# A two-layer hybrid network on one core: the loops of all stages written out, and the normalisation of the MoE route stages moved from VectorE to ScalarE

## The reference

```python
x = x + rwkv(layernorm(x))            # L0_attn_a: token shift, low-rank mixes, recurrence over time
x = x + moe(layernorm(x))             # L0_ffn: 8 experts, each takes its top 65 tokens of a sequence
x = x + retention(layernorm(x))       # L0_attn_b: 16 heads, decay, gated
x = x + moe(layernorm(x))
x = x + rnn(layernorm(x))             # L1_attn_a: h = tanh(h @ A.T + bx_t), 256 steps
x = x + ffn(layernorm(x))             # L1_ffn: 128 -> 512 -> 128, gelu
x = x + wkv(layernorm(x))             # L1_attn_b: 1024 channels, cumulative sums
x = x + ffn(layernorm(x))

def _layernorm(x, axis=-1, eps=1e-05):
    m = jnp.mean(x, axis=axis, keepdims=True)
    v = jnp.var(x, axis=axis, keepdims=True)
    return (x - m) / jnp.sqrt(v + eps)

scores = softmax(einsum('bsd,ed->bse', x, router_w))      # of the MoE block
gate_vals, sel_idx = top_k(swapaxes(scores, 1, 2), 65)
```

## Time and profile before

| | us |
|---|---|
| median of 3 runs | 3743.26 (3743.24 to 3748.52) |
| the profiled execution, own time | 3741.77 |
| its span, first to last instruction | 3740.0 |
| mean granted TensorE clock | 0.879 |

### The profile page before, as it was taken

How to read it: one execution, slowest core, us unless ns; L and a number is a source line. 1 busy time by engine, 2 the same in 40 slices (tenths; PEclk the granted TensorE clock), 3 DMA queues, 4 the chain that set the end, 5 groups by cost and what they waited for, 6 DMA issues and landing times. The chain is left out here.

```text
span 3740.0 us, 56099 instructions
## 1 busy us (share of the span) xinstructions
PE 3132.0 (84%) x16680; PEld 2027.5 (54%) x16680; DVE 2491.7 (67%) x5841; ACT 1666.5 (45%) x3563; POOL 1202.9 (32%) x1203
## 2 busy tenths in 40 slices
PE   4777776599987399999649996887979999999989
PEld 2333334488853144444548885676745555555557
DVE  5888777544469677777564444201569999999975
ACT  1222221233333299999413332221436666666644
POOL 2333332000013277777310000100224444444432
PEclk9878876699988599999769998555989999999999
DMA  3000001111013200000220000000000000000001
GB/s 106 1 0 0 0 0 52 63 44 43 0 40 110 65 28 27 27 27 19 69 76 35 35 17 1 1 0 25 0 1 1 1 0 0 0 0 0 0 1 45
DMA packets 106211, 89.75 MB, mean 24 GB/s; under 512 B 15789, under 2 KB 95923, under 8 KB 103776
## 3 DMA queue, kind: packets, MB, share of 16 engines
q1 hardware_dynamic: 104784, 87.13, 7.2%
q10 hardware_dynamic: 1296, 1.02, 0.1%
HBM read 57.68 MB, written 30.15 MB: 23 GB/s over the span
## 5 line engine op out<-in xcount | busy, mean ns | idle before, releaser
L2228 ACT ACTIVATE m_x_hT<-m_x_hid,wm_b 128x260 f32<-128x260 f32 x512 | 242.3, 478 | 435.3 <-PE m_x_hid L2150 435.3
L1112 DVE TENSOR_REDUCE c_tM<-c_tpa 128x2 f32<-128x512 f32 x512 | 331.8, 681 | 129.7 <-PE c_tpa L1014 128.7
L1229 POOL TENSOR_TENSOR c_tE<-c_tE,c_tDm 128x256 f32<-128x256 f32 x512 | 372.6, 728 | 139.6 <-ACT c_tE L1189 124.9
L1189 ACT ACTIVATE c_tE<-c_tpb 128x512 f32<-128x512 f32 x512 | 310.1, 607 | 43.2 <-PE c_tpb L1031 43.2
L2150 PE MATMUL m_x_hid<-m_x_xg,wm_w 128*128 128x260 f32 x1024 | 306.6, 387 | 8.4 <-ACT m_x_hT L2228 6.1
L2158 PE MATMUL m_x_yp<-m_x_hT,wm_w 128*128 128x260 f32 x1024 | 299.9, 382 | 0.0
L79 POOL TENSOR_TENSOR rstd<-vareps,neg_half 128x4 f32<-128x4 f32 x105 | 112.7, 1073 | 550.7 <-DVE vareps L68 550.7
L1565 POOL TENSOR_TENSOR b_wkv<-b_at,b_rec 128x512 f32<-128x512 f32 x128 | 163.0, 1274 | 314.1 <-DVE b_rec L1501 314.1
L1014 PE MATMUL c_tpa<-c_tK,c_Qm 96*128 96x256 f16 x1024 | 205.2, 283 | 48.8 <-DMA c_Qm<-aug_d 34.2
L72 DVE TENSOR_SCALAR xn<-X,mean,rstd 128x128 f32 (+1 forms) x420 | 162.9, 449 | 108.2 <-POOL rstd L79 108.2
L2075 DVE TENSOR_SCALAR m_x_yT<-m_x_yp,wm_b 128x260 f32<-128x260 f32 x128 | 62.5, 489 | 251.3 <-PE m_x_yp L2158 251.3
(11 more groups left out here) (296 smaller groups left out, 7371.1 us busy)
## 6 DMA issues: line engine op xcount, KB each, us to landing
m_x_ir<-idx_d SPq DMA_DIRECT2D x16, 1040.0 KB, 6.7
xn_d<-xn SPq DMA_DIRECT2D x32, 256.0 KB, 2.3
m_x_xs<-xn_d SPq DMA_DIRECT2D x16, 512.0 KB, 4.1
c_tK<-k_d SPq DMA_DIRECT2D x32, 192.0 KB
c_Qm<-q_d SPq DMA_DIRECT2D x128, 48.0 KB
wm_w<-in_m_w SPq DMA_DIRECT2D x2, 2048.0 KB, 10.2
gate_d<-c_pgate SPq DMA_DIRECT2D x16, 256.0 KB
q_d<-c_phi SPq DMA_DIRECT2D x32, 128.0 KB
```

The source lines that it names most:

```text
L1112: nc.vector.tensor_reduce(out=M[:, u % 2, 2 * h:2 * h + 2], in_=pa[:, h % 2], axis=AX.X, op=ALU.max).then_inc(s["max_done"], 1)
L1189: nc.scalar.activation(E[:, h % 8].rearrange("p a q -> p (a q)"), pb[:, h % 2, :], ACT.Exp).then_inc(s["exp_done"], 1)
L1229: nc.gpsimd.tensor_tensor(diag, diag, Dm[:, u % 2, h:h + 1, :].to_broadcast([P, 2, P]), ALU.mult).then_inc(s["dmul_done"], 1)
L2228: nc.scalar.activation(hT[:, e % 2, j, :], hid[:, c % 2, 0:QW], ACT.Gelu, bias=w["m_b1"][:, c:c + 1]).then_inc(s["gelu_done"], 1)
```

## The change

All 29 `Fori` loops become Python loops, so every engine's code is written out. And in the route stage, besides:

- ScalarE normalises: `activation(Identity, scale=rstd, bias=shift)` with shift = -mean * rstd, four to a group, in the order evac(g), normalise(g + 2);
- VectorE only does `moments`, for all 16 groups one after another; the mean comes out negated;
- GpSimd works out shift behind the power, and now waits before the power until ScalarE has normalised group g - 2, whose slot it overwrites;
- moments(g) waits for `shift_done` of group g - 2 in place of `xn_done`; ScalarE's normalise(g) waits for shift(g), for the turn of group g - 2 and for the store of group g - 2.

```diff
-            with dve.Fori(1, NG // 2) as i:
+            for i in range(1, NG // 2):
...
@@ stage_route @@
+        shift = sb("shift", [P, 2, GT])
...
             def moments(g, u):
 
                 at_least(dve, s["ln_tick"], g * MOMENTS)
-                at_least(dve, s["xn_done"], (g - 1) * GT)
+                at_least(dve, s["shift_done"], g - 1)
...
-                nc.vector.tensor_scalar(mean[:, u, :], mean[:, u, :], 0.5, None, ALU.mult).then_inc(s["ln_tick"], 1)
+                nc.vector.tensor_scalar(mean[:, u, :], mean[:, u, :], -0.5, None, ALU.mult).then_inc(s["ln_tick"], 1)
...
-            def normalise(g, u, wait):
-                if wait:
-                    dve.wait_ge(s["turned"], g - 1)
-                    dve.wait_ge(stored[u], (g - u) * 8)
-                dve.wait_ge(s["ln_rstd"], g + 1)
-                for i in range(GT):
-                    nc.vector.tensor_scalar(k.xn[:, u, i, :], k.X[:, g * GT + i, :], mean[:, u, i:i + 1], rstd[:, u, i:i + 1],
-                                            ALU.subtract, ALU.mult).then_inc(s["xn_done"], 1)
-
-            moments(0, 0)
-            for u in range(2):
-                moments(u + 1, 1 - u)
-                normalise(u, u, False)
-            with dve.Fori(1, NG // 2) as i:
-                for u in range(2):
-                    g = i * 2 + u
-                    moments(g + 1, 1 - u)
-                    normalise(g, u, True)
+            for g in range(NG):
+                moments(g, g % 2)
...
                     pool.wait_ge(s["ln_tick"], (g + 1) * MOMENTS)
+                    at_least(pool, s["xn_done"], (g - 1) * GT)
                     nc.gpsimd.tensor_tensor(rstd[:, u, :], vareps[:, u, :], k.neg_half[:], ALU.pow).then_inc(s["ln_rstd"], 1)
+                    pool.wait_ge(s["ln_rstd"], g + 1)
+                    nc.gpsimd.tensor_tensor(shift[:, u, :], mean[:, u, :], rstd[:, u, :], ALU.mult).then_inc(s["shift_done"], 1)
...
-            evac(0, 0, False)
-            evac(1, 1, False)
-            with act.Fori(1, NG // 2) as i:
-                for u in range(2):
-                    evac(i * 2 + u, u, True)
+
+            def normalise(g, u):
+                act.wait_ge(s["shift_done"], g + 1)
+                at_least(act, s["turned"], g - 1)
+                at_least(act, stored[u], (g - u) * 8)
+                for i in range(GT):
+                    nc.scalar.activation(k.xn[:, u, i, :], k.X[:, g * GT + i, :], ACT.Identity, scale=rstd[:, u, i:i + 1],
+                                         bias=shift[:, u, i:i + 1]).then_inc(s["xn_done"], 1)
+
+            normalise(0, 0)
+            normalise(1, 1)
+            for g in range(NG):
+                evac(g, g % 2, g > 1)
+                if g + 2 < NG:
+                    normalise(g + 2, g % 2)
```

More of the change, by code:

```diff
@@ L243, in _ @@
             down(1, 1, False)
-            with pe.Fori(1, NG // 2) as i:
+            for i in range(1, NG // 2):
                 for u in range(2):
@@ L488, in _ @@
             iteration(1, 1, False)
-            with pool.Fori(1, NG // 2) as i:
+            for i in range(1, NG // 2):
                 for u in range(2):
@@ L782, in _ @@
             one(0)
-            with pool.Fori(1, NG) as g:
+            for g in range(1, NG):
                 one(g)
@@ L1091, in _ @@
                 iteration(0, u, first=(u == 0), second=(u == 1))
-            with pe.Fori(1, NI - 1) as i:
+            for i in range(1, NI - 1):
                 for u in range(NB):
@@ L1233, in _ @@
                 iteration(0, u)
-            with pool.Fori(1, NI - 1) as i:
+            for i in range(1, NI - 1):
                 for u in range(NB):
@@ L1806, in stage_route @@
     with ExitStack() as ctx:
-        s = sems(nc, ctx, tag, "ln_tick ln_rstd xn_done turned xT_ready logits stored0 stored1 soft exp_done rows work top0 top1 out")
+        s = sems(nc, ctx, tag, "ln_tick shift_done ln_rstd xn_done turned xT_ready logits stored0 stored1 soft exp_done rows work top0 top1 out")
         ps = lambda name, shape: ctx.enter_context(nc.psum_tensor(tag + name, shape, F32))
@@ L1832, in _ @@
         def _(sp):
-            with sp.Fori(0, NG // 2) as i:
+            for i in range(0, NG // 2):
                 for u in range(2):
@@ L1923, in _ @@
         def _(pool):
-            with pool.Fori(0, NG // 2) as i:
+            for i in range(0, NG // 2):
                 for u in range(2):
@@ L1947, in _ @@
             turn_in(1, 1, False)
-            with pe.Fori(0, NG // 2 - 1) as i:
+            for i in range(0, NG // 2 - 1):
                 for u in range(2):
@@ L2047, in _ @@
             low_part(1, 1)
-            with pool.Fori(1, NQ // 2) as i:
+            for i in range(1, NQ // 2):
                 for u in range(2):
@@ L2119, in _ @@
             quad(1, 1, False, False)
-            with dve.Fori(1, NQ // 2 - 1) as i:
+            for i in range(1, NQ // 2 - 1):
                 for u in range(2):
@@ L2205, in _ @@
             quad(1, 1, False, False)
-            with pe.Fori(1, NQ // 2 - 1) as i:
+            for i in range(1, NQ // 2 - 1):
                 for u in range(2):
@@ L2233, in _ @@
             quad(1, 1, False, False)
-            with act.Fori(1, NQ // 2 - 1) as i:
+            for i in range(1, NQ // 2 - 1):
                 for u in range(2):
```

9 lines of the change are left out of this document (4 added, 5 removed).

## The result

The changed kernel takes **3714.3 us** (median of 4 runs, 3713.1 to 3716.3) against 3745.7 for the kernel before (3743.2 to 3748.5, 4 runs): ratio 0.9916, 95% interval 0.9901 to 0.9932. Predicted were 3722 us (3704 to 3735) and faster with a chance of 0.86. The sign and the range held; the gain between the medians is 31 us where 20 were forecast.

A forecast was written before the change was run, and what follows sets the result against it. VectorE was taken to pace the route stage at 3.07 us a group, TensorE to bound wkv and FFN. Route 14, project 2.9, experts 1.3 and rwkv 2 sum to 20 us off 3741.8: 3722 us, range 3704 to 3735.

The forecast's parts named there:

- Route: Both route stages: pace falls from VectorE's 3.07 us a group to TensorE's 2.62; 7 us a stage, 14 us.
- TensorE's pitch: Route stage: turns 0.91 plus logits 1.71 make 2.62 us a group, the true pitch some 0.05 less.
- Project: Retention project: written out 9.33 us a group against 9.54 looped; 2.9 us gained.
- Experts: Both experts stages: written out 44.46 us a quad against 44.61 looped; 1.3 us gained.
- Attend and FFN: Retention attend, 15.68 us looped and written out, and both FFN stages, bound by TensorE: 0 gained.
- wkv: wkv stage: TensorE is busy 97% and its queue hides the loop arithmetic; 0 gained.
- rwkv: rwkv stage, bound by a chain through four engines at 34.13 us an iteration: 2 us gained from written-out loops.
- A: Route stages: TensorE's clock rises, ScalarE's 2.2 us sets the pace, 13 us more, 3709 us; chance 8%.
- B: rwkv stage: leaves its 34.13 us period for a mean near 33.3, 11 us more, 3711 us; chance 15%.
- C: Route: ScalarE or GpSimd binds at 2.9 us a group, 3730 us (8%); if rwkv also loses, 3737 (7%).
- E: Loops: removing registers shows only in peeled prologues and rwkv gives nothing, 3729 us; within the forecast's range, no separate chance.
- D: Written-out code: 76 new instruction fetches stall TensorE, 71 us more, 3793 us; with every second one 3757; chance 5%.

The follow-up runs named there:

- before + 64: The kernel before with 64 one-column memsets added in VectorE's idle time in the recurrence stage: 3782.6 us (2 runs).

## Why the prediction was right, and where it was off

**Route, 7 us a stage: right mechanism, mis-sized, 9.4 and 9.1.** VectorE set the pace before and TensorE does now, at a clock of 0.50. The term that was off most is TensorE's pitch: "2.62", with 0.05 taken off for the modelled end of the last matmul. It measured 2.45, 0.17 less. From start to start, a turn is 0.89 us and the logits 1.56, where the forecast had 0.91 and, to a modelled end, 1.71. The 0.12 a group that were missed are 1.8 us a stage; another 0.5 is the lead to the first turn, which grew by 0.35 us and not by 0.9 (4.49 before, 4.84 now). Together they are the 2.4 by which 9.4 exceeds 7. The idle time told it as well: 8.0 us of waits over 16 groups are 0.5 a group, 3.07 - 0.5 = 2.57, and there too the ends are modelled. Of the parts, ScalarE's normalisation was 0.40 an operation and measured 0.484; two overlap by a little, so a group is 1.65 us as forecast (1.6). GpSimd's multiply was 0.4 and measured 0.21, inside its bounds. The new waits cost 0.6 us of TensorE's time, as forecast (0.85). What the prediction did not separate: some 2.6 us of each stage come from writing out the old code, not from moving the normalisation.

**Project, 2.9: right** (3.0; 9.33 in every group), and VectorE's loop is its cause.

**Experts, 1.3: a small term of the right sign in its intervals and lost in the stages' heads.** 44.64 became 44.42 in the middle quads, part of it TensorE's loop (44.55) and part ScalarE's (44.50). In whole the two stages changed by -2.2 and +1.9 us: from the maximum to the first y by -1.3 and +1.6, and one more interval of the second stage is 1.1 us long (45.56 once), as heads vary from run to run.

**Attend and FFN, 0: right.** 15.68 and 7.45 in the steady intervals.

**wkv, 0: wrong, 5.9 us.** The failed step is that TensorE, busy for 97%, has a queue that "hides the arithmetic". Per group TensorE is busy 50.5 us before and 50.6 after, and the group went from 51.58 to 51.16. The 1 us a group in which TensorE was not busy was waiting (1.9 us in two groups, for b_wkv), and part of it was VectorE's arithmetic, late by 0.42. The argument needed 100%, or a pair of intervals as in project; the loop's prologue in wkv was not read for it.

**rwkv, 2: wrong, nothing gained and a little lost.** The failed step is the price of 0.2 us taken over from project. The interval is 34.13 with loops and without, as the prediction's own sentence "the fixed period may swallow it" allowed. Of the +3.3 in the table 2.5 are not the change: before and before + 64 have the same rwkv code, and the second iteration began 2.5 us later in the latter's profile. The end of the stage did change. In all seven kernels whose VectorE code is written out here the last two intervals are 34.21 and 35.68, in all six with VectorE's loop 34.13. There the granted clock of TensorE rose later: 0.55 from 558 to 562 us in the changed kernel, against 0.96 at the same point of the iteration with VectorE's loops back (556.4 to 560.4). The rest of the stage is then 1.3 us shorter (24.9 in place of 26.2), so little of it counts. What fixes the period, and why its end shifts, was not tried.

**The rivals.** A (clock rises) did not happen; lifted by hand the clock fell back within the stage. The section on the PE-mode transpose in "TensorE: Matmul & The Clock Gate" of the Trainium skill, cited for this, agrees with the trace: TensorE was busy with turns and short logits for all of 622 to 655 us, at 0.50. B, C and E did not happen (rwkv kept its period, ScalarE and GpSimd did not bind, project went to 9.33 in every group). D, exposed fetches, did not in the changed kernel: 136 fetches on TensorE's queue (forecast 140) with no steady interval longer for them (attend shows 15.88 once, and 15.48 behind it). The forecast counted that queue alone; the one that feeds VectorE went from 67 packets to 117. But its mechanism is real, and where it cost much it hit a loop, not the written-out code. "Runtime: NRT & Kernel Launch" of the Trainium skill, section "Instruction fetch mechanics", calls a branch the thing that breaks the prefetch. The prediction set this aside, since "no looped interval here shows such a break". The intervals of before did not, and with 64 more instructions ahead of the loop they do, for 36 us.

**The sum.** Forecast 20, measured 25 between the profiled executions: route 4.5 more, wkv 6 more, rwkv 5 less (2.5 of them not the change), experts 1 less. The medians are 31 apart; the other 6 us are how the two profiled executions lie against their medians, and were not traced. The two large errors had the same sign; the likeliest number lay 8 us beside the result, and the range held it thanks to rivals that did not come true. That much was luck. And the parts do not simply add. The route edit alone was worth 0 or 20 us in a kernel with loops, by where its code length put VectorE's wkv loop. Written-out loops took that lottery away.

## What to carry to other kernels

Before an edit is judged by its time, compare the steady intervals of the stages that it didn't touch. A loop as long as this one, 2.5 fetch packets, can be refetched in every round when unrelated code ahead of it grows or shrinks: the signs are an idle "issue" at its first instruction and a count of instruction fetches that goes with the rounds. Half a packet of padding tells, and cures it until the code ahead changes again; with the loop written out, wkv's groups stayed at 51.16 in all seven kernels. An engine at 97% can still have a path through the others, as TensorE here, so price a loop's register arithmetic there by intervals with and without, not by the busy share.

## What the runs showed of the hardware that was not expected

- A loop of 321 VectorE instructions (20.5 KB at 64 bytes) ran from what had been fetched, or was fetched five times 8 KB a round, by a shift of 64 instructions; a shift of 128 changed nothing. The refetch cost 2 us at the branch and 2.2 to 6.1 us in a round of 103 us. TensorE's loop in the same stage, 836 instructions a round and fetched in packets of 16 KB, stayed at 1 or 2 packets in all five kernels.
- With matmuls put ahead of the turns, TensorE's granted clock was 1.00 when the turns began, 0.60 from 626 to 628 us and 0.50 for the rest of the stage, with TensorE fully busy on transposes and matmuls of 8 columns.
